# Adding the two picks' first-layer rows on VectorE in front of the second layer of a two-pick feed-forward

## The chip, the core and the metric

The kernel runs on one core of one Trainium2 chip. The metric is the device time of one execution in microseconds, as the median of several executions. The core's engines are named as the profile names them: PE is TensorE (PEld its weight loads), DVE is VectorE, ACT is ScalarE, POOL is GpSimd, SP is SyncE.

## The reference

The reference works on 2048 tokens of 128 features and runs four sub-layers in a row, each as x = x + layernorm(f(layernorm(x))): a linear attention, a feed-forward with two picked low-rank experts, an attention over 16 heads that keeps the 64 largest scores of each row, and a mixture of eight gated experts. Two of them matter here. The first feed-forward:

```python
top_v, top_i = jax.lax.top_k(scores, TOP_K)          # TOP_K = 2
val_sum = top_v.sum(axis=-1)
for e in range(E):
    count = (top_i == e).sum(axis=-1).astype(hidden_states.dtype)
    gate = count * val_sum
    inter = hidden @ wi.T + bi + (hidden @ lora_A[e].T) @ lora_B[e].T
    h = jax.nn.relu(inter)
    expert_out = h @ wo.T + bo
    out = out + gate[..., None] * expert_out
```

Both picks of a token carry the same gate and share `wo` and `bo`, so the output is val_sum * (h1 @ wo.T + h2 @ wo.T + 2 * bo), where h1 and h2 are the 512 hidden features of the first and of the second pick. The attention that comes after it selects by a threshold:

```python
topk_vals = jax.lax.top_k(dots, K)[0]                # K = 64
thresh = topk_vals[..., -1:]
dots = jnp.where(dots < thresh, NEG_INF, dots)
```

## The kernel before

All arithmetic named here is in f32 except where another type is given. The tokens are 16 tiles of 128, and the first feed-forward takes them in four blocks `b` of four tiles. One program per engine is written out by hand, and each runs its instructions in the order of the code. Results go through eight PSUM banks in a ring: the list `fills` (from `plan_fills`) names every filling of a bank in order, PE fills, and ACT or DVE empties. PE waits for the bank's last user (`open_fill`).

**First layer** (PE lines 891 and 892, function `mids`). For each block there are eight fillings `("mid", b, n)`. Number n stands for pick n // 4 and for hidden features 128 * (n % 4) and on. Each is two products over 512 tokens, and ACT drains it with bias and relu (line 579, recorded as L501, the line of the helper `drain`) into `mid[:, b % 2, n, :]`, a slice of the buffer R. The order before is n = 0, 1, ..., 7: first the four of pick 0, then the four of pick 1. Every f32 matmul stands as two matmul instructions in the profile.

**Second layer** (PE lines 902 and 903). PE waits until ACT has drained `("mid", b, 7)`, and then makes for each of the four tiles eight products of 128 x 128 x 128, which run over both picks and accumulate in PSUM, and one product of a single row that adds 2 * bo.

**Normalisation** (DVE lines 1239 to 1252). DVE scales the block by val_sum (L1242), normalises it, adds it to X (L1250) and normalises X again for the next sub-layer. ACT gives the two square roots; in ACT's order they stand ahead of the third and the sixth first-layer drain of the following block. PE transposes the normalised block behind the next block's second layer (L761), and the last block's at the end.

**The attention behind it** works in 64 groups k: tile t = k // 4, and four heads i of the sixteen, 4 * (k % 4) + i. A group is four score rows for each of 128 tokens, 16 + 128 * (t + 1) scores wide. DVE finds for every row the 56th largest of 128 candidates in f16 (`pivots`, whose first instruction is L1286) and sets a cut a little below it. ACT counts the scores above the cut; if these are 56 to 64, the threshold is the cut or one of the eight largest scores below it. A row is in doubt where the count lies outside, or where a score equals the cut bit for bit:

```python
mark(dve.scalar_tensor_tensor(out=tie[:, :], in0=r9[:, :, 1], scalar=-BIG_, in1=cutb[:, k % 2, :],
                              op0=ALU.mult, op1=ALU.is_le))
...
    mark(dve.scalar_tensor_tensor(out=doubt[:, GU * g:GU * g + GU], in0=th[rows_g, :], scalar=0.0,
                                  in1=tie[rows_g, :], op0=ALU.is_equal, op1=ALU.max))
...
with dve.If(doubtful != 0):
    settle(k)
```

One doubtful row among the 512 of a group sends DVE into `settle(k)`. It goes over the four heads in a loop and repeats an exact search for the head in doubt: a copy (L1365), then eight times MAX8 (L1368, L1372) with MATCH_REPLACE8 between them (L1370). DVE releases ACT and PE for the group's values only afterwards (line 1428, `s_lose`).

Of the kernel before, what the change touches and what calls it, by code (L numbers as in the profile page):

```python
# [5 lines left out]
ALU = mybir.AluOpType  # L6
# [4 lines left out]
P = 128  # L11
# [19 lines left out]
HALF = 2.0 ** 23  # L31
CUT = 56
CONSTS = 4 + 2 * E0 + 9
GU = 4
NG = UNITS // GU
F16 = mybir.dt.float16
# [44 lines left out]
def plan_fills():  # L81
    f = Fills()
    for n in ("wi", "wo", "loraB", "loraA_gate"):
        f.add(n, "act")
    for b in range(6):
        f.add(("wqkv", b), "act")
    f.add("memk", "act")
    f.add("memv", "act")
    for b in range(4):
        f.add(("h", 0, b), "act")  # L90
    for b in range(8):
        f.add(("kv", b), "dve")
    for b in range(4):
        f.add(("q", b), "dve")
    f.add("memscore", "act")
    f.add(("G", 0), "act")
    f.add(("G", 1), "act")
    f.add("kvsum", "dve")
    for b in range(8):
        f.add(("att", b), "dve")  # L100
    f.add(("G", 2), "act")
    f.add(("G", 3), "act")
    for g in range(4):
        f.add(("M", g), "act")
    for g in range(4):
        f.add(("MV", g), "act")
    for b in range(4):
        f.add(("h", 1, b), "act")
    f.add("logit0", "dve")
    for b in range(4):  # L110
        f.add(("lowrank", b), "dve")
    for k in range(2):
        for b in range(4):
            f.add(("pick", k, b), "act")
    for b in range(4):
        for n in range(8):
            f.add(("mid", b, n), "act")
        f.add(("ffn0", b), "dve")
        if b:
            f.add(("h", 2, b - 1), "act")  # L120
    f.add(("h", 2, 3), "act")
    return f
# [55 lines left out]
def build(nc, out, x, Wqkv, bqkv, wi, bi, wo, bo0, loraA, loraB, gate_w, gate_b, Wq, Wkv, Wo, bo1, pre, mem_k, mem_v,  # L178
          ln_w, ln_b, router_w, gw1, uw1, dw1, shg, shu, shd):
    fills, ffills, order = plan_fills(), plan_ffn1(), ffn1_order()  # L180
    with ExitStack() as ctx:
# [3 lines left out]
        def sem(name):  # L185
            return ctx.enter_context(nc.semaphore(name))
# [130 lines left out]
        s_drain_a = sem("s_drain_a")  # L317
# [5 lines left out]
        s_pk, s_pq = sem("s_pk"), sem("s_pq")  # L323
        s_kvm = sem("s_kvm")
        s_logit, s_exp = sem("s_logit"), sem("s_exp")
        s_pick = sem("s_pick")
        s_pre, s_WkS, s_mkS, s_G = sem("s_pre"), sem("s_WkS"), sem("s_mkS"), sem("s_G")
        s_out = sem("s_out")

# [160 lines left out]
        def _(act):  # L490
# [76 lines left out]
                drain(("h", 2, b), hT[:, 512 * b:512 * b + 512])  # L567

            for b in range(4):
                for n in range(8):  # L570
                    if n == 0 and b >= 2:

                        act.wait_ge(s_fill, fills.index(("ffn0", b - 2)) + 1)
                        drain_h2(b - 2)
                    if b and n == 2:
                        sqrt(2 + 2 * b, 4 * b - 4, 4 * b)
                    if b and n == 5:
                        sqrt(3 + 2 * b, 4 * b - 4, 4 * b)
                    drain(("mid", b, n), mid[:, b % 2, n, :], ACT.Relu, bias=bcol[:, 1 + n % 4:2 + n % 4])
            drain_h2(2)  # L580
# [169 lines left out]
        def _(pe):  # L750
# [134 lines left out]
            pe.wait_ge(s_drain_a, fills.drained(fills.index(("pick", 1, 3))))  # L885

            def mids(b):
                for n in range(8):
                    k = open_fill(("mid", b, n))
                    f = n % 4  # L890
                    pe.matmul(k, wiT[:, P * f:P * f + P], hT[:, 512 * b:512 * b + 512], start=True, stop=False)
                    pe.matmul(k, lBT[:, P * f:P * f + P], pickT[:, n // 4, 512 * b:512 * b + 512], start=False, stop=True)\
                        .then_inc(s_fill, 1)

            for b in range(4):
                mids(b)
                pe.wait_ge(s_drain_a, fills.drained(fills.index(("mid", b, 7))))
                k = open_fill(("ffn0", b))
                for i in range(4):
                    o = k[:, P * i:P * i + P]  # L900
                    for n in range(8):
                        pe.matmul(o, mid[:, b % 2, n, P * i:P * i + P], woT[:, n % 4, :], start=(n == 0), stop=False)
                    last = pe.matmul(o, tworow[:, :], rows[:, 264:392], start=False, stop=True)
                last.then_inc(s_fill, 1)
                if b:
                    pe.wait_ge(s_rows, 2 + b)
                    turn_block(("h", 2), b - 1)
# [180 lines left out]
        def _(dve):  # L1088
# [136 lines left out]
            for n in range(2):  # L1225
# [10 lines left out]
                    dve.wait_ge(s_drain_v, fills.drained(fills.index(("lowrank", 3))))  # L1236
                dve.sem_inc(s_pick, 1)
            for b in range(4):
                k = drained(("ffn0", b))
                for i in range(4):  # L1240
                    t = 4 * b + i
                    ins = dve.tensor_scalar(Y[:, t, :], k[:, P * i:P * i + P], sm[:, 2, t:t + 1], None, ALU.mult)  # L1242
                    if i < 3:
                        mark(ins)
                ins.then_inc(s_drain_v, 1)
                dve.wait_ge(s_dve, done[0])
                dve.wait_ge(s_drain_v, fills.drained(fills.index(("ffn0", b))))
                tiles = (4 * b, 4 * b + 4)
                normalize(Y, T1r, *tiles)
                link(dve.tensor_tensor(X[:, tiles[0]:tiles[1], :], X[:, tiles[0]:tiles[1], :], T1r[:, tiles[0]:tiles[1], :], ALU.add))  # L1250
                normalize(X, Y, *tiles)
                dve.sem_inc(s_rows, 1)
# [308 lines left out]
```

## Time and profile before

| | us |
|---|---|
| median of three executions | 2591.53 |
| lowest and highest | 2587.34, 2593.87 |
| the profiled execution | 2588.66 |
| its span (first to last instruction) | 2586.9 |

The span runs through the sub-layers one behind the other: the linear attention to about 125 us, the first feed-forward from 138 to 246 us, the selecting attention to about 2370 us, and the second feed-forward to the end. In the first feed-forward one engine's work follows another's by semaphore. In a timeline row the first number is the start, the second the duration, and a bracket holds the engine's idle time before it and what ended that. A run of instructions of one kind stands as one row with its count.

### The profile page before, as it was taken

Reading aid. Unit: us, or ns where it says so; the run is one execution under the profiler, and the core shown is the slowest. Engines: PE = TensorE matmul, PEld = TensorE weight load, DVE = VectorE, ACT = ScalarE, POOL = GpSimd, SP = SyncE. Lnnn points to the kernel's source line nnn. Section 1 sums busy time; section 2 is a strip of 40 time slices with the busy share of each in tenths; the row PEclk is TensorE's granted clock in tenths of the full one; section 3 lists DMA queues with packets and bytes.
Section 4 is the critical chain, followed back from the end, with each engine's and each line's share of the span. In section 5 each row is a group of like instructions: output and inputs, shape, how many; then the busy total and the mean of one; then the engine's idle time right before and its main releaser. Section 6 shows DMA issues by size and latency. Waiting matters only on the chain.

```text
span 2586.9 us, 34852 instructions
## 1 busy us (share of the span) xinstructions
PE 2154.9 (83%) x10150; PEld 1278.2 (49%) x10150; DVE 2145.0 (83%) x8999; ACT 1571.0 (61%) x2340; POOL 592.9 (23%) x459
## 2 busy tenths in 40 slices
PE   5998466777788478888989989999993999988997
PEld 3755343344444244545545545555551555555665
DVE  5523999999999899999998988988988998987445
ACT  2132345566666367777777777878782888874221
POOL 4200022222323122222333313313130423131000
PEclk9898667898989789999999999999996999988999
DMA  3000000000000000000000000000000000002000
GB/s 72 1 1 17 1 1 1 1 1 1 1 1 1 1 1 1 1 1 1 1 1 1 1 1 1 1 1 1 1 1 0 1 1 1 1 11 64 1 1 17
DMA packets 18211, 13.78 MB, mean 5 GB/s; under 512 B 6987, under 2 KB 15956, under 8 KB 18004
## 3 DMA queue, kind: packets, MB, share of 16 engines
q1 hardware_dynamic: 13824, 8.92, 1.3%
q10 hardware_dynamic: 4180, 2.50, 0.4%
q8 instruction: 81, 1.33, 0.2%
q14 instruction: 126, 1.03, 0.1%
HBM read 9.32 MB, written 2.10 MB: 4 GB/s over the span
## 4 chain that ended last, share of the span: by engine, by line
PE 45%; DVE 36%; ACT 10%; issue 4%; POOL 2%; DVEq 2%; SPq 1%; DMA 0%; ACTq 0%; POOLq 0%
PE bank L975 11%; DVE cand L1273 10%; PE bank L959 7%; PE bank L943 7%; DVE F L1344 5%; PE bank L1047 5%; ACT R L659 5%; PE bank L960 3%; DVE W L1303 3%; DVE W L1302 2%; PE bank L1055 2%; ACT R L609 2%; DVE R L1331 2%; DVE r L1333 2%; DVE r L1328 2%
## 5 line engine op out<-in xcount | busy, mean ns | idle before, releaser
L943 PE MATMUL bank<-hT,qT 128*128 128x512 f32 (+3 forms) x1280 | 591.4, 599 | 211.0 <-ACT R L609 122.0
L1273 DVE MAX8 cand<-R 128x8 f32<-128x12 f32 (+15 forms) x4096 | 671.6, 222 | 5.6 <-ACT R L609 5.2
L975 PE MATMUL bank<-WP,Y 128*128 128x512 f32 x1088 | 584.7, 631 | 0.5 <-ACT WP L666 0.2
L465 POOL TENSOR_TENSOR X<-R,X 128x144 f32<-128x144 f32 (+15 forms) x64 | 164.1, 2564 | 1675.3 <-ACT X L652 1675.3
L943 PEld LDWEIGHTS bank<-hT,qT 128*128 128x128 f32 x1280 | 244.9, 211 | 477.0 <-issue 197.5
L959 PE MATMUL bank<-ident,R 128*128 128x128 f32 x2176 | 436.2, 284 | 21.3 <-ACT R L659 15.9
L659 ACT ACTIVATE R<-R,negm 128x144 f32<-128x144 f32 (+15 forms) x256 | 309.6, 1211 | 186.0 <-DVEq L1428 186.0
L960 PE MATMUL bank<-nidentb,F 128*128 128x128 bf16 x2176 | 404.9, 222 | 0.0
L666 ACT ACTIVATE WP<-bank 128x512 f32<-128x512 f32 x544 | 320.7, 593 | 119.1 <-PE bank L960 108.3
L959 PEld LDWEIGHTS bank<-ident,R 128*128 128x128 f32 x2176 | 311.8, 143 | 149.9 <-issue 91.6
L609 ACT ACTIVATE R<-bank 128x1024 f32<-128x1024 f32 (+7 forms) x384 | 290.5, 771 | 137.8 <-PE bank L943 70.6
L636 ACT ACTIVATE signs<-R,cutb 128x144 int8<-128x144 f32 (+15 forms) x256 | 309.9, 1210 | 3.6
L960 PEld LDWEIGHTS bank<-nidentb,F 128*128 128x128 bf16 x2176 | 229.4, 105 | 103.2 <-issue 103.0
L1303 DVE TENSOR_TENSOR W<-W 128x256 f16<-128x256 f16 x768 | 216.2, 282 | 0.0
L1302 DVE TENSOR_TENSOR W<-W 128x256 f16<-128x256 f16 x768 | 208.1, 271 | 0.4
L975 PEld LDWEIGHTS bank<-WP,Y 128*128 128x128 f32 x1088 | 173.2, 195 | 53.4 <-issue 31.3
L1344 DVE TENSOR_SCALAR F<-R,thr 128x144 bf16<-128x144 f32 (+15 forms) x256 | 197.0, 771 | 2.1
L1331 DVE SCALAR_TENSOR_TENSOR R<-R,r 128x144 f32<-128x144 f32 (+15 forms) x128 | 183.9, 1437 | 4.5
L1333 DVE MAX8 r<-R 128x8 f32<-128x144 f32 (+15 forms) x128 | 167.9, 1312 | 4.4
L465 POOL TENSOR_TENSOR R<-R 128x144 f32<-128x144 f32 (+15 forms) x64 | 162.3, 2536 | 4.6 <-ACT R L652 4.4
L925 PE MATMUL bank<-hT,G 128*128 128x128 f32 x512 | 85.8, 319 | 87.3 <-ACT R L609 86.0
L652 ACT ACTIVATE X<-R,cutb 128x144 f32<-128x144 f32 (+15 forms) x64 | 77.6, 1213 | 91.4 <-DVE cutb L1317 91.4
(243 smaller groups left out, 2715.6 us busy)
## 6 DMA issues: line engine op xcount, KB each, us to landing
R<-in_L_attn_Wkv ACTq DMA_DIRECT2D x2, 512.0 KB, 8.4
out<-X SPq DMA_DIRECT2D x1, 1024.0 KB, 5.1
R<-in_L_ffn_gate_w SPq DMA_DIRECT2D x1, 1024.0 KB, 9.1
R<-in_L_ffn_up_w SPq DMA_DIRECT2D x1, 1024.0 KB, 11.6
out<-X SPq DMA_DIRECT2D x4, 256.0 KB, 2.3
R<-in_L_attn_Wq ACTq DMA_DIRECT2D x1, 512.0 KB, 6.8
WP<-in_L_attn_Wo ACTq DMA_DIRECT2D x1, 512.0 KB, 10.6
R<-in_L_ffn_wi SPq DMA_DIRECT2D x1, 256.0 KB
```

Source lines behind the costliest of these rows:

```text
L465: pool.tensor_tensor(OV[i - 2][:, 0:n], S[:, k % NS, i, 0:n], OV[i - 2][:, 0:n], ALU.subtract)\
L609: act.activation(S[:, k % NS, i, MEM + SC * c:MEM + SC * c + w], src[:, 0:w], ACT.Copy)\
L636: act.activation(signs[:, 0:n], S[:, k % NS, i, 0:n], ACT.Sign, bias=cutb[:, k % 2, i:i + 1], scale=BIG_, accum_out=cnt[:, k % 2, i:i + 1] ...
L659: act.activation(row, row, ACT.Exp, bias=negm[:, k % 2, i:i + 1], scale=1.0 / LOW).then_inc(s_prob, 1)
L666: act.activation(PT[:, b % 4, :], bank[4 + n % 2], ACT.Relu).then_inc(s_tdrain, 1)
L943: last = pe.matmul(to, qT[:, k % 2, i, :], hT[:, a:b], start=True, stop=b < n, skip_group_check=True)
L959: pe.transpose(to[:, P * i:P * i + P], S[:, k % NS, i, blk], ident[:, :])
L960: last = pe.matmul(to[:, P * i:P * i + P], F[:, i, blk], nidentb[:, :], start=False, stop=True, skip_group_check=True)
L975: pe.matmul(bank[6], Y[:, j, :], PT[:, (blocks_before(k) + j) % 4, :], start=(j == 0), stop=(j == k // 4))\
L1273: mark(dve.max(cand[:, :, c, i], lists(S[:, k % NS, i, 0:n], n, c)))
L1303: step = beside(step, dve.tensor_tensor(dst[:, :, 1, :], src[:, :, 0, :], src[:, :, 1, :], ALU.min))
L1344: mark(dve.tensor_scalar(F[:, i, 0:n], S[:, k % NS, i, 0:n], thr[:, i:i + 1], 4.0, ALU.is_lt, ALU.mult))
```

## The change

The two picks' hidden rows are added before the second layer: mid[n] += mid[n + 4] for n = 0 to 3, by four additions of 128 x 512 on DVE for each block. The second layer then runs over n = 0 to 3 alone, four products a tile where eight were. The bias row stays. So that additions can be made while the first layer still runs, the order of the first layer's fillings becomes 0, 4, 1, 5, 2, 6, 3, 7, in the plan, on ACT and on PE; ACT's two square roots keep their places by position. A new semaphore `s_pair` counts the additions, and PE waits for it in place of ACT's last drain.

```diff
+PAIRED = (0, 4, 1, 5, 2, 6, 3, 7)
...
     for b in range(4):
-        for n in range(8):
+        for n in PAIRED:
             f.add(("mid", b, n), "act")
...
             for b in range(4):
-                for n in range(8):
-                    if n == 0 and b >= 2:
+                for place_, n in enumerate(PAIRED):
+                    if place_ == 0 and b >= 2:
 
                         act.wait_ge(s_fill, fills.index(("ffn0", b - 2)) + 1)
                         drain_h2(b - 2)
-                    if b and n == 2:
+                    if b and place_ == 2:
                         sqrt(2 + 2 * b, 4 * b - 4, 4 * b)
-                    if b and n == 5:
+                    if b and place_ == 5:
                         sqrt(3 + 2 * b, 4 * b - 4, 4 * b)
...
             def mids(b):
-                for n in range(8):
+                for n in PAIRED:
                     k = open_fill(("mid", b, n))
...
             for b in range(4):
                 mids(b)
-                pe.wait_ge(s_drain_a, fills.drained(fills.index(("mid", b, 7))))
                 k = open_fill(("ffn0", b))
+                pe.wait_ge(s_pair, 4 * b + 4)
                 for i in range(4):
                     o = k[:, P * i:P * i + P]
-                    for n in range(8):
-                        pe.matmul(o, mid[:, b % 2, n, P * i:P * i + P], woT[:, n % 4, :], start=(n == 0), stop=False)
+                    for n in range(4):
+                        pe.matmul(o, mid[:, b % 2, n, P * i:P * i + P], woT[:, n, :], start=(n == 0), stop=False)
                     last = pe.matmul(o, tworow[:, :], rows[:, 264:392], start=False, stop=True)
...
             for b in range(4):
+                for n in range(4):
+                    dve.wait_ge(s_drain_a, fills.drained(fills.index(("mid", b, n + 4))))
+                    dve.tensor_tensor(mid[:, b % 2, n, :], mid[:, b % 2, n, :], mid[:, b % 2, n + 4, :], ALU.add)\
+                        .then_inc(s_pair, 1)
                 k = drained(("ffn0", b))
```

Lines of the changed kernel are up to five higher than before; L902 becomes L903 and L1250 becomes L1255.

PE, the last filling of block 0's first layer, its second layer and the first filling of block 1 (WP holds the weights `woT`, R holds `mid`, Zs and qT the bias row). Before:

```order
L891 MATMUL bank<-hT,WP 128x512 [waits s_drain_a]
L892 MATMUL bank<-R,WP 128x512
L902 MATMUL bank<-WP,R 128x128 [waits s_drain_a]
L902 MATMUL bank<-WP,R 128x128 x7
L903 MATMUL bank<-Zs,qT 128x128
L902 MATMUL bank<-WP,R 128x128 x8
L903 MATMUL bank<-Zs,qT 128x128
```

Changed:

```order
L892 MATMUL bank<-hT,WP 128x512 [waits s_drain_a]
L893 MATMUL bank<-R,WP 128x512
L903 MATMUL bank<-WP,R 128x128 [waits s_pair,s_drain_a]
L903 MATMUL bank<-WP,R 128x128 x3
L904 MATMUL bank<-Zs,qT 128x128
L903 MATMUL bank<-WP,R 128x128 x4
L904 MATMUL bank<-Zs,qT 128x128
```

Four products of each tile are gone, and the first one waits for `s_pair`.

DVE, from the end of block 0's normalisation to the start of block 1's. Before:

```order
L1115 RECIPROCAL rstd<-std 128x4 [waits s_std]
L1117 TENSOR_SCALAR Y<-X,mv,rstd 128x128 [waits s_dve]
L1117 TENSOR_SCALAR Y<-X,mv,rstd 128x128 x3
L1242 TENSOR_SCALAR Y<-bank,sm 128x128 [waits s_dve,s_fill]
L1242 TENSOR_SCALAR Y<-bank,sm 128x128 x3
```

Changed:

```order
L1116 RECIPROCAL rstd<-std 128x4 [waits s_std]
L1118 TENSOR_SCALAR Y<-X,mv,rstd 128x128 [waits s_dve]
L1118 TENSOR_SCALAR Y<-X,mv,rstd 128x128 x3
L1242 TENSOR_TENSOR R<-R 128x512 [waits s_dve,s_drain_a]
L1242 TENSOR_TENSOR R<-R 128x512 [waits s_drain_a] x3
L1247 TENSOR_SCALAR Y<-bank,sm 128x128 [waits s_fill]
L1247 TENSOR_SCALAR Y<-bank,sm 128x128 x3
```

The four additions of block 1 stand behind all of block 0's normalisation and ahead of block 1's.

## Rows read from the trace of the kernel before

**Rows 1.** Page, part 4: the chain that ended last.

```profile
PE 45%; DVE 36%; ACT 10%; issue 4%; POOL 2%; DVEq 2%; SPq 1%; DMA 0%; ACTq 0%; POOLq 0%
```

**Rows 2.** Windows of the second layer, a first layer, the last normalisation: busy, PEclk.

```profile
core 0: us, PE busy (x) PEld busy (x) DVE busy (x) ACT busy (x) POOL busy (x), PEclk, DMA share, GB/s
152.00:162.40 10.40, 9.65 (x73) 8.69 (x73) 0.00 (x0) 0.69 (x1) 0.00 (x0) 1.00 0.00 0
212.00:226.00 14.00, 13.83 (x33) 5.83 (x32) 6.79 (x32) 5.72 (x11) 0.00 (x0) 1.00 0.00 0
236.00:246.00 10.00, 1.96 (x10) 1.21 (x9) 7.39 (x36) 1.27 (x4) 0.00 (x0) 0.77 0.04 12
```

**Rows 3.** Timeline, end of block 0's first layer: start us, us, instruction.

```profile
152.01 0.69 ACT L501 ACTIVATE R<-bank,bcol 128x512 f32<-128x512 f32 x1 [1.03 <-PE bank L892]
...
152.75 2.05 PE L902 MATMUL bank<-WP,R 128*128 128x128 f32 x16 [0.78 <-ACT R L501]
...
154.73 0.48 PE L903 MATMUL bank<-Zs,qT 1*128 1x128 f32 x2
...
155.15 2.05 PE L902 MATMUL bank<-WP,R 128*128 128x128 f32 x16
```

**Rows 4.** Instruction groups by line, first feed-forward (137 to 247 us).

```profile
L902 PE MATMUL bank<-WP,R 128*128 128x128 f32 x256 | 32.8, 281 | 3.1 <-ACT R L501 3.1
...
L1250 DVE TENSOR_TENSOR X<-X,R 128x512 f32<-128x512 f32 x4 | 2.8, 693 | 0.1
```

**Rows 5.** Timeline, block 2's normalisation on DVE and block 3's last drain.

```profile
211.55 1.12 DVE L1242 TENSOR_SCALAR Y<-bank,sm 128x128 f32<-128x128 f32 x4 [13.44 <-PE bank L903]
...
221.75 1.11 DVE L1117 TENSOR_SCALAR Y<-X,mv,rstd 128x128 f32<-128x128 f32 x4
...
225.87 0.69 ACT L501 ACTIVATE R<-bank,bcol 128x512 f32<-128x512 f32 x1 [1.03 <-PE bank L892]
```

**Rows 6.** Timeline, DVE to PE after the last normalisation.

```profile
243.36 1.11 DVE L1117 TENSOR_SCALAR Y<-X,mv,rstd 128x128 f32<-128x128 f32 x4
...
244.59 1.12 PE L761 MATMUL bank<-ident,Y 128*128 128x128 f32 x4 [7.74 <-DVEq L1252]
```

**Rows 7.** Timeline, one kind of product at either clock level.

```profile
246.96 2.04 PE L925 MATMUL bank<-hT,G 128*128 128x128 f32 x8 [1.26 <-ACT MV L587]
...
256.47 1.16 PE L925 MATMUL bank<-hT,G 128*128 128x128 f32 x8
```

**Rows 8.** Timeline, L1286 opens each group's pivot search.

```profile
822.76 0.27 DVE L1286 TENSOR_REDUCE top<-cand 128x4 f32<-128x64 f32 x1 [0.38 <-DVE F L1344]
...
850.44 0.27 DVE L1286 TENSOR_REDUCE top<-cand 128x4 f32<-128x64 f32 x1 [0.68 <-DVE F L1344]
...
905.91 0.27 DVE L1286 TENSOR_REDUCE top<-cand 128x4 f32<-128x64 f32 x1 [3.90 <-issue]
...
936.81 0.27 DVE L1286 TENSOR_REDUCE top<-cand 128x4 f32<-128x64 f32 x1 [0.40 <-DVE F L1344]
...
966.08 0.27 DVE L1286 TENSOR_REDUCE top<-cand 128x4 f32<-128x64 f32 x1 [0.67 <-DVE F L1344]
...
1902.71 0.27 DVE L1286 TENSOR_REDUCE top<-cand 128x4 f32<-128x64 f32 x1
...
1987.19 0.27 DVE L1286 TENSOR_REDUCE top<-cand 128x4 f32<-128x64 f32 x1 [1.55 <-issue]
...
2029.94 0.27 DVE L1286 TENSOR_REDUCE top<-cand 128x4 f32<-128x64 f32 x1 [0.21 <-DVE F L1344]
```

**Rows 9.** Timeline, DVE and ACT in the exact search of tile 6.

```profile
880.33 0.64 DVE L1365 COPY R<-R 128x912 f32 x1 [1.10 <-issue]
...
905.85 1.06 ACT L659 ACTIVATE R<-R,negm 128x912 f32<-128x912 f32 x1 [29.80 <-DVEq L1428]
```

**Rows 10.** Timeline, the copy of the exact search of tile 13.

```profile
1949.08 1.10 DVE L1365 COPY R<-R 128x1808 f32 x1 [3.50 <-issue]
```

**Rows 11.** One source line: the exact search's MAX8, all its executions.

```profile
L1368 DVE MAX8 r<-R x14: 1110/1578/2046, 881.1 to 1977.7; 128x8 f32<-128x912 f32 x7, 128x8 f32<-128x1808 f32 x7
```

More of the change, by code:

```diff
@@ L325, in build @@
         s_logit, s_exp = sem("s_logit"), sem("s_exp")
-        s_pick = sem("s_pick")
+        s_pick, s_pair = sem("s_pick"), sem("s_pair")
         s_pre, s_WkS, s_mkS, s_G = sem("s_pre"), sem("s_WkS"), sem("s_mkS"), sem("s_G")
```

## The prediction

> **What bounds the kernel now.** I read the page first. The chain that ended last is PE for 45% and DVE for 36% of the span [rows 1]; it goes through the first feed-forward on PE, so time taken out there comes off the end. The windows of that stage say how: in the second layer PE is busy 9.65 of 10.40 us and DVE not at all, in a first layer PE is busy 13.83 of 14.00, DVE 6.79, ACT 5.72, all at granted clock 1.00, the level of 2.4 GHz [rows 2]. So PE is the bound in all four blocks and DVE is idle through each second layer. Behind it, in the selecting attention, DVE and its short releases to ACT and PE set the pace. There the starts of the pivot search (L1286) are some 28 to 43 us apart, with two exceptions: 55.5 us where group 26 (tile 6) is worked, and 84.5 us where group 55 (tile 13) is [rows 8]. Both hold one exact search: the source line has 14 MAX8, seven 912 wide and seven 1808 wide [rows 11].
>
> **Part 1, the products that go.** A tile's eight products are 16 recorded instructions that run from 152.75 to 154.73, where the bias row begins: 1.98 us, 0.124 each; a tile follows the one before after 2.40 us [rows 3]. There are 256 of them in all [rows 4], 128 go: 16 tiles x 8 x 0.124 = 15.8 us, all on PE's path. A tile then takes 1.41 us and a block's second layer 5.6 instead of 9.6.
>
> **Part 2, the additions that come.** 16 additions of 128 x 512 in f32 on DVE. The same form in the same stage, both operands in SBUF and in place, is L1250: 693 ns [rows 4]. The first three of a block are made while PE still runs the first layer and cost nothing, if DVE is free. In block 0 it is. In block 3 DVE's normalisation of block 2 starts at 211.55 and ends at 222.86, ACT's last drain ends at 226.56 [rows 5]; three additions take 2.1 us, so they are done by 225.0, with 1.6 us to spare. The fourth waits for the last drain and lies on the path. Today PE starts 0.05 us after that drain (152.70 to 152.75, [rows 3]). The new path is drain, 0.05, addition 0.69, and then 0.05 to PE, or 0.12 if DVE's release costs what the last normalisation's does (244.47 to 244.59, [rows 6]). That is 0.74 to 0.81 more a block; I take 0.78, since either release may apply, and 3.1 us for four. The lower bound is the addition alone, 0.69, since it needs the last drain and nothing can hide it; the upper one is all four additions behind the drain, 2.9 us a block and 11.6 in all.
>
> **Part 3, what is moved.** The new order of the first layer has the same 64 products on the same banks' ring, drained by the same ACT instructions. The square roots keep their positions, and DVE reaches the variances as early as before, since the additions stand behind the normalisation. PE's wait for the normalised block (L761) is already fulfilled when the second layer may start, as the additions follow that normalisation on DVE. Behind the new wait on PE stand only the second layer and what needs it. After the last block DVE has been idle and the closing normalisation is as long as before. Nothing here: 0.
>
> First feed-forward: 15.8 - 3.1 = 12.7 us off.
>
> **Part 4, the bits.** The change alters the rounding of the second layer: f32 sums of h1 + h2 go into four products instead of eight products into one sum. Every score of the attention behind it then moves in its last bits, and one branch hangs on bits: a row is in doubt where a score equals the cut exactly. I recomputed the sub-layers from the reference's inputs in double precision, with the kernel's lists, f16 pivot and f32 cut. Among some 32,000 rows just one has a count outside 56 to 64: tile 13, head 14, token 46, with 65 scores above the cut, the nearest score 6e-4 of the cut away. That is a third head of its group, and the trace agrees: in tile 13's search the copy starts 3.50 us after the flags, in tile 6's after 1.10 [rows 9, 10], so tile 13 skips two heads and tile 6 none. Rounding can't move that row. The search of tile 6 has no such row; but 16 rows have a score within 1e-6 of the cut, one of them in tile 6, head 8, token 81: group 26, first head, just where the trace has its search. So I read it as a tie in the last bit, and a tie doesn't outlive a new rounding but by chance.
>
> Its price is read from the starts of L1286. Group 26 takes 905.91 - 850.44 = 55.47 us, group 25 took 27.68: 27.8. Group 27 then takes 30.90 where group 28, in a wider tile, takes 29.27 [rows 8]: up to 1.6 more. ACT had stood idle 29.80 us for DVE's release [rows 9], so nothing hides it. I take 28.5 between 27.8 and 29.4. Tile 13's search costs 84.48 - 42.75 = 41.7 by the same rows, so a search costs about 2.0 us more for each tile further on: 22 in tile 3, 38 in tile 11, 40 in tile 12.
>
> How many new ties? In 60 redraws with random errors of 2e-7 on the normalised rows (plain f32 departs from double by 3.4e-7 there, and adding the picks first shifts the f32 rows by 1.7e-7), 33 had no tie, 19 one, 8 two, the old one came back once, the 65-row was there each time. Of the new ones two thirds lie in tiles 11 and 12.
>
> **The sum.** 2588.66 - 12.7 - 28.5 = 2547.5 for the profiled execution, which lies 2.9 below the median; against the median 2591.53 - 41.2 = 2550.3. I forecast 2550.
>
> **The rivals.** *One new tie.* The same draw brings one search: 2550 plus 20 to 44, in tile 11 or 12 2588 to 2590, which would look like no change though the stage is 12.7 shorter. For it speaks the count of near rows, 16 before the change too.
>
> *Two new ties, the slower side.* One search costs at most 28 + 9 x 2 = 46, which is less than the 49 that lie between 2550 and 0.3% above the median; from two on in the wide tiles it is slower: in 11 and 12, 2550 + 78 = 2628. It would show as more than 14 MAX8 on that line.
>
> *The bits don't decide.* The tile 6 search stays, because it comes from something else or falls on the same bit again: 2591.5 - 12.7 = 2578.8. For it speaks only that the trace names no cause; against it that the tie's place agrees in tile, group and head.
>
> *DVE becomes the late one.* If additions ran at twice 693 ns beside PE's and ACT's work on the same buffer, three would end at 222.86 + 4.2 = 227.0 instead of before 226.56, and each block would cost about 1.9 more than summed: in all up to 7 us, 2557. Against it: L1250 already runs beside ACT's drains and takes 693.
>
> *The clock.* PE's pause before each second layer grows from 0.78 [rows 3] to 1.6 us and the burst behind it halves. The four pauses of 0.78 left the granted clock at 1.00; it fell after the pause of 7.74 us at the end of the stage [rows 2, 6]. At the lower level, 1.2 GHz, eight equal records take 2.04 us instead of 1.16 [rows 7], a factor of 1.76; four second layers of 5.6 us would cost 17 more: 2567. I hold that the level stays. The Trainium skill, "TensorE: Matmul & The Clock Gate", section "A second HAM failure mode: psum-queue depth-cycling", speaks against the change here: small pauses between groups of products, as PE cycles through its banks, can swing the clock between its levels. By that rule the time is that rival's, by the row of the pauses it is the forecast; the trace has no pause of 1.6 us in this stage.
>
> *It doesn't do what it says.* The order shows eight products a tile before and four after, so the removal is real.
>
> **How the numbers follow.** Forecast 2550 (no tie anywhere): 0.53. One new tie, 2568 to 2595: 0.30. Two or more: 0.12. Search of tile 6 stays, 2579: 0.05. The DVE and the clock rival have 0.04 and 0.03 beside any of these, and move the forecast without changing its sign. A measurement of this kernel can tell about 0.3%, 7.8 us, from no change. Faster by more: 0.53 + 0.05, and of the single ties those in tiles up to 8, 0.05: 0.63. Within: the single ties further on, 0.24. Slower: two ties and a little of the single ones, 0.13. The range from 2545 (every cost at its lower end, and the scatter of the runs) to 2595 (one tie in a wide tile) leaves out the double ties. Single numbers in between are less likely than either end. The forecast's own range is 2545 to 2558.
>
> **What would show it.** In the changed trace: the products of the second layer are 128 records of 0.28 us mean, tiles 1.41 us apart; PE's wait before each second layer about 1.55 us, now for DVE; DVE's additions 16 x 0.69; the next sub-layer's first product 12.7 us earlier than 246.96; granted clock 1.00 through the blocks. Then MAX8 on the exact search's line seven times, 1808 wide only, and group 26 about 28 us long. If that line has 14 or more of other widths, the draw went the other way; if the same 912 wide search is there, my reading of the tie is wrong. If the stage itself is not 12 to 13 us shorter, part 1 or part 2 is.

## The result, and the profile after

| | us |
|---|---|
| changed kernel, median of four executions | 2566.53 (2555.21 to 2566.71) |
| kernel before, median of four | 2592.70 (2587.34 to 2596.04) |
| ratio, with 95% interval | 0.9894 (0.9874 to 0.9915) |
| profiled execution, changed | 2566.43, span 2564.7 |

The changed kernel is 1.1% faster. That is the forecast's direction and inside its whole range of 2545 to 2595, but 16 us above the forecast of 2550 and outside 2545 to 2558, the range that went with no tie. The profiled execution is 22.2 us shorter than that of before. Hardly any of it comes out of the feed-forward that was changed.

The changed stage first. The windows below cover the whole stage, from the first product of the first layer to the closing transposes, before and after. A row gives the stretch, its length, the busy time and the instructions of PE, PEld, DVE, ACT and POOL, and then PE's granted clock, where 1.00 is the level of 2.4 GHz and 0.50 that of 1.2 GHz:

```profile
137.97:244.59 106.62, 95.77 (x429) 59.66 (x429) 28.97 (x132) 26.14 (x44) 0.00 (x0) 0.99 0.00 1
```

```profile
140.26:245.71 105.45, 91.79 (x301) 52.45 (x301) 39.50 (x148) 26.14 (x44) 0.00 (x0) 0.86 0.00 0
```

It took 106.62 us and takes 105.45. PE has 128 matmul records fewer and is busy only 4 us less, since the granted clock is 0.86 in the mean where it was 0.99. Windows of the changed kernel show where the clock was lost:

```profile
140.00:154.00 14.00, 13.74 (x32) 6.00 (x32) 2.07 (x3) 5.02 (x8) 0.00 (x0) 1.00 0.00 0
154.00:158.00 4.00, 2.40 (x15) 1.93 (x15) 0.69 (x1) 0.69 (x1) 0.00 (x0) 0.96 0.00 0
157.80:171.30 13.50, 13.50 (x36) 8.56 (x35) 2.55 (x13) 0.69 (x1) 0.00 (x0) 0.50 0.00 0
158.00:170.00 12.00, 12.00 (x34) 8.03 (x33) 2.55 (x13) 0.69 (x1) 0.00 (x0) 0.50 0.00 0
170.00:184.00 14.00, 12.40 (x28) 5.12 (x27) 7.28 (x24) 6.39 (x10) 0.00 (x0) 0.95 0.00 0
206.00:228.00 22.00, 20.41 (x78) 11.46 (x78) 9.83 (x37) 6.28 (x11) 0.00 (x0) 1.00 0.00 1
228.00:246.00 18.00, 10.72 (x46) 8.74 (x46) 7.24 (x33) 1.01 (x3) 0.00 (x0) 0.54 0.00 0
```

Behind the pause of block 0 PE runs at 0.50 for more than 13 us, through most of the second layer and the first two of the eight fillings of block 1's first layer. The level does not fall in the pause but some 2 us behind it, when PE is busy again. Behind the pause of block 3 it falls once more. Blocks 1 and 2 keep 1.00. Before the change no block lost it:

```profile
138.00:241.00 103.00, 95.73 (x428) 59.62 (x428) 25.91 (x118) 25.94 (x43) 0.00 (x0) 1.00 0.00 1
```

The timeline of block 0's second layer, which answers to [rows 3]:

```profile
154.30 0.69 ACT L502 ACTIVATE R<-bank,bcol 128x512 f32<-128x512 f32 x1 [1.03 <-PE bank L893]
155.02 0.69 DVE L1242 TENSOR_TENSOR R<-R 128x512 f32<-128x512 f32 x1 [2.74 <-ACT R L502]
...
155.86 1.13 PE L903 MATMUL bank<-WP,R 128*128 128x128 f32 x8 [1.60 <-DVE R L1242]
...
157.33 1.75 PE L903 MATMUL bank<-WP,R 128*128 128x128 f32 x8
...
159.74 2.08 PE L903 MATMUL bank<-WP,R 128*128 128x128 f32 x8
```

and of block 2's, which kept the clock:

```profile
205.81 1.13 PE L903 MATMUL bank<-WP,R 128*128 128x128 f32 x8 [1.60 <-DVE R L1242]
...
207.28 1.16 PE L903 MATMUL bank<-WP,R 128*128 128x128 f32 x8
...
208.78 1.16 PE L903 MATMUL bank<-WP,R 128*128 128x128 f32 x8
```

The pause is 1.60 us, 0.82 more than the 0.78 of before. The four products of a tile take 1.16 us at the upper level and 2.08 at the lower. Block 2 gives the cost without a fall: a tile follows the one before after 1.50 us.

The fall's price follows from the starts of the second layers: 155.86, 183.84, 205.81 and 227.77. Block 1 to block 2 is 21.97 us. Block 0 to block 1 would be 0.39 shorter without a fall, since no transposes stand between (before: 24.36 against 24.75), so 21.58; it took 27.98: 6.4 lost. Block 3's second layer took 9.54 to its transposes where block 2's took 5.97: 3.6 lost. Together these are 10.0. The pause before the second layer and that layer itself are the same in all four blocks. What picks blocks 0 and 3 therefore lies elsewhere, and no run here shows it.

Then the selecting attention. The exact search's MAX8 stands seven times where it stood 14 times [rows 11], and the starts of L1291, the L1286 of before, show no long group there any more (compare [rows 8]):

```profile
L1373 DVE MAX8 r<-R x7: 2044/2044/2045, 1928.1 to 1955.4; 128x8 f32<-128x1808 f32 x7
```

```profile
852.28 0.27 DVE L1291 TENSOR_REDUCE top<-cand 128x4 f32<-128x64 f32 x1 [0.39 <-DVE F L1349]
...
880.00 0.27 DVE L1291 TENSOR_REDUCE top<-cand 128x4 f32<-128x64 f32 x1 [0.38 <-DVE F L1349]
...
908.07 0.27 DVE L1291 TENSOR_REDUCE top<-cand 128x4 f32<-128x64 f32 x1 [0.69 <-DVE F L1349]
```

From the first two, group 26 takes 27.72 us where it took 55.47, and group 27 takes 28.07 where it took 30.90: 30.6 us off in these two.

Elsewhere groups 36 to 41 are 6.5 us longer in sum. Group 36 and group 40, before and after:

```profile
1182.61:1215.40 32.79, 28.09 (x141) 16.16 (x139) 30.98 (x127) 24.90 (x37) 9.79 (x6) 1.00 0.00 1
...
1317.11:1352.31 35.20, 31.82 (x151) 17.93 (x149) 32.59 (x128) 26.97 (x38) 10.54 (x6) 0.95 0.00 1
```

```profile
1153.60:1188.08 34.48, 29.78 (x141) 16.75 (x139) 30.98 (x128) 25.03 (x37) 9.70 (x6) 0.95 0.00 1
...
1291.02:1328.06 37.04, 33.27 (x151) 18.21 (x149) 32.70 (x127) 27.07 (x38) 10.48 (x6) 0.91 0.00 1
```

The work is the same; PE was granted 0.05 less of its clock in group 36 and 0.04 less in group 40. This is not the change's doing. The two kernels below that leave the stage as before ("Only the bits" and "Only the cut") also take 211.4 us for the six groups, where the profile of before has 205.3 and that of the changed kernel 211.7. The account of the 22.2 us is then: 2.3 later at the stage's start (137.97 to 140.26), 1.2 off in the stage, 30.6 off at the search, 6.5 back in groups 36 to 41, and 0.8 back as the sum over the rest, where single groups differ by 1.6 less to 2.6 more.

### The profile page after: what moved, and what is told of

It is laid out like the page before. It is cut to its first block, busy times and chain, and to the rows that moved or that the text cites. A ratio compares the mean times of both kernels' runs of the same rounds, so it can differ in the third digit from the quotient of the medians.

```text
span 2564.7 us, 34512 instructions
## 1 busy us (share of the span) xinstructions
PE 2148.9 (84%) x10022; PEld 1267.2 (49%) x10022; DVE 2135.9 (83%) x8985; ACT 1570.3 (61%) x2340; POOL 592.5 (23%) x459
## 4 chain that ended last, share of the span: by engine, by line
PE 42%; DVE 35%; ACT 10%; issue 4%; POOL 2%; DVEq 1%; ACTq 0%; POOLq 0%
PE bank L976 10%; DVE cand L1278 10%; PE bank L960 7%; PE bank L944 7%; DVE F L1349 5%; ACT R L660 5%; PE bank L1048 5%; PE bank L961 3%; DVE W L1308 3%; DVE W L1307 2%; PE bank L1056 2%; ACT R L610 2%; DVE R L1336 2%; DVE r L1338 2%; DVE r L1333 2%
## 5 line engine op out<-in xcount | busy, mean ns | idle before, releaser
L466 POOL TENSOR_TENSOR X<-R,X 128x144 f32<-128x144 f32 (+15 forms) x64 | 163.7, 2558 | 1653.7 <-ACT X L653 1653.7
```

Of the source, the lines that this page charges most:

```text
L466: pool.tensor_tensor(OV[i - 2][:, 0:n], S[:, k % NS, i, 0:n], OV[i - 2][:, 0:n], ALU.subtract)\
```

## The experiments

Two questions: what lowers the granted clock, and what decides the exact search. "Stage" is always the time from the first layer's first product to the closing transposes of that kernel's profile.

### The additions without the shorter second layer

```diff
-    dve.tensor_tensor(mid[:, b % 2, n, :], mid[:, b % 2, n, :], mid[:, b % 2, n + 4, :], ALU.add)\
+    dve.tensor_tensor(T2[:, 512 * n:512 * n + 512], mid[:, b % 2, n, :], mid[:, b % 2, n + 4, :], ALU.add)\
...
-    for n in range(4):
-        pe.matmul(o, mid[:, b % 2, n, P * i:P * i + P], woT[:, n, :], start=(n == 0), stop=False)
+    for n in range(8):
+        pe.matmul(o, mid[:, b % 2, n, P * i:P * i + P], woT[:, n % 4, :], start=(n == 0), stop=False)
```

> The changed kernel with all eight products of a tile in the second layer again, in the old order 0 to 7; the additions are made as in the changed kernel and waited for, but written to scratch space that nobody reads. So PE's pause before each second layer is the changed kernel's (1.60 us), the burst behind it (9.6 us) and the bits are those of before. Stage below is from the first first-layer product to the start of the closing transposes: 106.6 us before, 105.5 changed. Theory A (the longer pause lets the granted clock fall): 106.6 + 4 x 0.82 = 109.9 if it holds, 3.6 to 6 us more for each fall, so some executions of 114 to 120 and a scatter of 10 us between executions. Rival B (the halved burst lets it fall): 109.9 every time, granted clock 1.00 in all four blocks. Theory on the search of tile 6 (a tie in the last bit): the old bits bring it back, 14 MAX8 on the exact search's line, group 26 about 55.5 us. Rival (timing or order brings it): 7 MAX8. Total 2591 + 3.3 = about 2595, with falls up to 2606.

The window of the stage, and the part of it up to the wait after the last block:

```profile
138.48:248.25 109.77, 95.64 (x428) 59.67 (x429) 39.53 (x148) 26.14 (x44) 0.00 (x0) 0.98 0.00 1
138.50:244.00 105.50, 95.63 (x428) 59.65 (x428) 35.83 (x133) 25.94 (x43) 0.00 (x0) 1.00 0.00 1
```

Stage 109.77 us, with four pauses of 1.59 to 1.60 us and no fall before the wait that follows the last block. The term of 0.78 to 0.81 us for each added wait is confirmed: 3.15 for four. The search of tile 6 is back, group 26 takes 58.12 us. So the timing of the changed kernel doesn't remove that search; its bits do. The median is 2594.34 against 2594.03 (ratio 0.9999, 0.9988 to 1.0009), so none of the 3.15 us more in the stage shows in the total; where it was given back stays open. The changed kernel lost its clock behind two of four such pauses, so one profile with none of four does not rule out that the long second layer, too, can lose it at this pause.

### Products that fill the pause

```diff
+    for n in range(6):
+        pe.matmul(k[:, 0:P], ident[:, :], woT[:, n % 4, :], start=True, stop=True, skip_group_check=True)
     pe.wait_ge(s_pair, 4 * b + 4)
```

> The changed kernel, with six products of 128 x 128 more on PE between the first and the second layer of each block, which stand ahead of the wait for the additions and whose result is overwritten. They fill the pause of 1.60 us (12 records of 0.124 = 1.49). Theory A: the granted clock stays at 1.00 in all four blocks, the stage takes 105.5 - 9.6 = about 96 us in every execution, total about 2556, with little scatter. Rival B (the short burst, not the pause): falls remain, the total stays near 2566 in most executions. Bits are the changed kernel's: 7 MAX8, all 1808 wide.

```profile
138.72:233.94 95.22, 86.81 (x348) 51.36 (x349) 39.53 (x148) 26.14 (x44) 0.00 (x0) 0.97 0.00 0
```

Stage 95.22 us, no fall, PE idle only 0.16 us before each second layer. Median 2552.61 (2548.95 to 2556.86), ratio to before 0.9839 (0.9825 to 0.9853). With 24 products more, the kernel is 14 us faster than the changed one; 10.2 us of it lie in the stage. The short second layer stayed, so it didn't lower the clock without the pause.

### Three pairs added, the fourth as two products

```diff
-    pe.wait_ge(s_pair, 4 * b + 4)
+    pe.wait_ge(s_drain_a, fills.drained(fills.index(("mid", b, 7))))
+    pe.wait_ge(s_pair, 3 * b + 3)
...
-    for n in range(4):
-        pe.matmul(o, mid[:, b % 2, n, P * i:P * i + P], woT[:, n, :], start=(n == 0), stop=False)
+    for n in (0, 1, 2, 3, 7):
+        pe.matmul(o, mid[:, b % 2, n, P * i:P * i + P], woT[:, n % 4, :], start=(n == 0), stop=False)
...
-    for n in range(4):
+    for n in range(3):
         dve.wait_ge(s_drain_a, fills.drained(fills.index(("mid", b, n + 4))))
```

> The changed kernel with only the first three pairs added; the fourth pair goes into the second layer as two products, so a tile has five products. PE waits for ACT's last drain, as before, and the additions are done by then. The pause is 0.78 us again, the burst about 6.7 us. Three products fewer at the measured 0.23 each (0.90 for four) are 0.68 a tile, 10.8 in all: stage 106.6 - 10.8 = about 96 us. Theory A: granted clock 1.00 through all blocks, every execution the same. Rival B: falls remain after the shorter burst. The bits are new: no search in tile 6, but a new tie somewhere with a chance of 4 in 10 at 20 to 44 us. Total 2554 to 2556 without one.

```profile
141.16:237.12 95.96, 84.92 (x332) 48.92 (x332) 36.77 (x144) 26.15 (x44) 0.00 (x0) 0.98 0.00 0
```

Stage 95.96 with pauses of 0.82 us and no fall, as expected: it is a second way to keep the clock. But the total is 2579.69 (2572.87 to 2584.43), since these bits bring a search too, in tile 6 again but in another group and head:

```profile
843.65 0.64 DVE L1371 COPY R<-R 128x912 f32 x1 [3.53 <-issue]
```

It stands in group 25 and starts 3.53 us after the flags, so two heads are skipped: the third head of that group, head 6. Before it was group 26 and the first head, head 8 [rows 9]. The old search was gone and a new one drawn, 27.8 us long: group 25 takes 55.45 us where it took 27.68 before.

### Only the bits

```diff
-    for n in range(8):
-        pe.matmul(o, mid[:, b % 2, n, P * i:P * i + P], woT[:, n % 4, :], start=(n == 0), stop=False)
+    for n in range(7, -1, -1):
+        pe.matmul(o, mid[:, b % 2, n, P * i:P * i + P], woT[:, n % 4, :], start=(n == 7), stop=False)
```

> The kernel before with one edit: the eight products of a tile are summed in the order 7 to 0. Same instructions, same waits, same timing of the stage (106.6 us); only the rounding differs. Theory (tie in the last bit): the search of tile 6 is gone, group 26 takes about 27.7 us, 7 MAX8 of 1808, total 2591 - 29 = 2562, unless a new tie stands elsewhere (4 in 10, 20 to 44 us, mostly in tiles 11 and 12). Rival (the search belongs to the timing, or to the data as such): 14 MAX8, 2591.

```profile
876.91 0.63 DVE L1365 COPY R<-R 128x912 f32 x1 [1.11 <-issue]
```

A miss: stage 106.62 as expected, but the search stays where it was, group 26, first head, and the total is 2592.28. Either the search wasn't a tie, or this change of rounding left that one score on the cut. The next run tells.

### Only the cut

```diff
-SLACK = 2.0 ** -14
+SLACK = 1.01 * 2.0 ** -14
```

> The kernel before with one constant changed: the slack by which the cut lies below the pivot is 1.01 times 2^-14. Bits of all scores and all timing are those of before; every cut moves by 6e-7, some hundred units in the last place, and no count changes by it except by accident. Theory (the search of tile 6 is a score equal to the cut): it is gone, group 26 takes about 27.7 us, total 29 lower, 2565, unless another tie stands at the moved cuts (4 in 10, 20 to 44 us). Rival (a count outside 56 to 64, or anything but an equality): 14 MAX8 as before, 2594. The search of tile 13 stays under both, as its count is off by a score 6e-4 of the cut away.

The exact search's MAX8 in that kernel:

```profile
L1368 DVE MAX8 r<-R x7: 2044/2044/2045, 1927.4 to 1954.8; 128x8 f32<-128x1808 f32 x7
```

The kernel before, with every score and every wait as it was and only the cuts moved by 6e-7, loses the search of tile 6 and is faster by as much: 2563.58 (2554.66 to 2566.91), ratio 0.9872 (0.9847 to 0.9896). The search of tile 13 stays. So some score of tile 6 lies within 6e-7 of its cut. That it equals the cut, and does not push a count over a bound, rests on the prediction's recomputation, which finds no count outside 56 to 64 in that tile. The recomputation was then repeated with the second layer's partial sums rounded in each order: the score of that row moves by 2 to 5 of its own last places. The products behind a score of 0.051 have magnitudes up to 0.87, where one f32 step is 16 of those last places. That the score lands on the same value again is therefore plausible, but only argued.

This kernel is also the fair partner of the changed one, since neither has the search of tile 6 and its stage is that of before (138.19 to 244.81, 106.62 us). Its 2563.58 against the changed kernel's 2566.53, and 0.9872 against 0.9894 with intervals that overlap, say that the changed feed-forward as it stands shows no gain of its own in the total.

### The shorter second layer without the pause

A burst is here the second layer of a block, PE's work behind a pause. So far neither the long pause before the long burst nor the short burst without the pause had lowered the clock. This suggested theory C: the two have to meet. This run has the short burst behind the short pause, with the second layer's products of pick 1 left out and no additions.

```diff
-    for n in range(8):
+    for n in range(4):
         pe.matmul(o, mid[:, b % 2, n, P * i:P * i + P], woT[:, n % 4, :], start=(n == 0), stop=False)
```

> The kernel before with the second layer's products of pick 1 left out, so four products a tile without any addition; PE waits only for ACT's last drain. The second layer's output lacks pick 1. Pause 0.78 us as before, burst 6.0 us as changed. The changed kernel lost its clock in blocks 0 and 3, the long pause with the long burst did not. Theory B (the short burst alone): the granted clock falls to 0.50 in some blocks, stage above 95 us. Theory C (pause of 1.60 and short burst have to meet): clock 1.00 in all blocks, stage 106.6 - 4 x 4 x 0.90 = 92.2 us, executions close together in that stage. The scores are other ones, so the exact searches say nothing here.

```profile
138.64:230.96 92.32, 81.47 (x300) 45.35 (x300) 28.98 (x132) 26.15 (x44) 0.00 (x0) 0.97 0.00 0
```

Stage 92.32 against 92.2 expected. The granted clock is 1.00 through all four blocks:

```profile
139.00:224.90 85.90, 81.11 (x300) 45.05 (x298) 23.82 (x108) 25.74 (x42) 0.00 (x0) 1.00 0.00 0
```

Behind pauses of 0.78 us the halved burst doesn't lower the clock, and four products of a tile are worth (106.62 - 92.32) / 16 = 0.89 us. The total, 2548.09, can't be compared, since the scores of the attention are other ones.

### A longer pause, with either burst

To the changed kernel, and then to the first experiment's kernel with eight products, one more addition is given to wait for:

```diff
-    pe.wait_ge(s_pair, 4 * b + 4)
+    pe.wait_ge(s_pair, 5 * b + 5)
...
+    dve.wait_ge(s_pair, 5 * b + 4)
+    dve.tensor_tensor(T2[:, 0:512], mid[:, b % 2, 3, :], mid[:, b % 2, 3, :], ALU.add).then_inc(s_pair, 1)
```

Short burst:

> The changed kernel with one more addition of 128 x 512 behind the last pair's, into scratch space, for which PE waits too. Pause about 2.35 us before each second layer, burst 6.0 us as changed; same bits as changed. Theory C: clock falls in more blocks than the changed kernel's two, three or all four; the stage would be 94.3 + 4 x 0.73 + 4 to 6 for each fall, 109 to 121 us, total 2572 to 2585, more than 2.9 above the changed kernel. Rival D (the two falls of the changed kernel's profile were chance and the pause's length within this range decides nothing): none to two falls, stage 97 to 109. 7 MAX8 by the bits.

Long burst:

> The kernel with the additions into scratch space and all eight products, with one addition more to wait for: pause 2.35 us, burst 9.6 us, bits of before. With the short burst this pause lost the clock in three of four blocks. Theory C (pause and short burst have to meet): clock 1.00 in all four blocks, stage 109.8 + 4 x 0.73 = 112.7 us. Rival A (the pause's length alone decides, and the one profile at 1.60 us with the long burst was luck): falls here too, stage 117 to 130 us. 14 MAX8 by the bits in either case.

Windows of the kernel with the short burst:

```profile
157.80:169.40 11.60, 11.60 (x35) 8.19 (x35) 2.55 (x13) 0.00 (x0) 0.00 (x0) 0.50 0.00 0
...
185.40:199.60 14.20, 14.20 (x46) 10.34 (x46) 2.55 (x13) 0.60 (x1) 0.00 (x0) 0.50 0.01 2
...
215.40:227.40 12.00, 12.00 (x44) 9.74 (x44) 1.49 (x6) 0.50 (x1) 0.00 (x0) 0.50 0.00 0
```

and of the kernel with the long burst:

```profile
154.40:166.00 11.60, 11.58 (x77) 9.66 (x78) 1.81 (x8) 0.01 (x1) 0.00 (x0) 1.00 0.01 1
...
181.00:184.00 3.00, 3.00 (x15) 2.78 (x15) 0.00 (x0) 0.00 (x0) 0.00 (x0) 0.52 0.00 0
184.00:200.00 16.00, 16.00 (x79) 10.70 (x80) 5.96 (x28) 3.44 (x6) 0.00 (x0) 1.00 0.00 1
...
235.10:241.80 6.70, 6.70 (x30) 6.16 (x29) 0.00 (x0) 0.00 (x0) 0.00 (x0) 0.50 0.01 2
```

With a pause of 2.32 us the clock falls behind all four pauses when the burst is short, each time for 12 us or more (the fourth fall shows in the closing part, 17.82 us where 14.3 would do); the stage is 122.15 us. The expectation of the long-burst run speaks of three blocks; the profile has all four. With the long burst the clock falls behind two of four pauses. In block 1 the level is back after some 3 us and in block 3 after some 7, both times inside the same burst. The first fall cost 1.6 us (block 1 to block 2 took 27.86, block 2 to block 3 26.26), the second 3.2 (12.73 us from the start of the second layer to its transposes, where block 2 took 9.55). Stage 117.44, where 112.7 was expected without falls. The total is 2602.29 (2599.85 to 2611.26), ratio 1.0032 (1.0018 to 1.0047), the only kernel here whose interval lies above that of before. So theory C, that pause and short burst must meet for a fall, was wrong in this form. The pause brings the fall. With the short burst behind it a fall lasted longer and cost more in every case here: 3.5 to 7.8 us with four products a tile, 1.6 to 3.2 with eight. The total of the short-burst kernel is 2567.70 (2558.40 to 2575.67). Its profiled execution is the slowest of them, 2575.67, only 9.2 us above the changed kernel's, though its stage is 16.7 us longer; the attention behind it, from the first to the last group, took 2008.9 us where the changed kernel's took 2015.5. Whether its quicker executions have fewer falls wasn't seen in a profile.

### The changed kernel again

> The changed kernel again, unchanged, to see how often the clock falls. Theory C: two levels of time about 11 us apart, 2555 and 2566, by whether the falls in blocks 0 and 3 happen, with more executions at the upper one; the profile shows which blocks. If all lie at 2566 the fall is fixed, if they spread evenly from 2555 to 2566 the falls are single events of 4 to 6 us each.

The stage in the profile is 105.56 us, with falls in blocks 0 and 3 again. Of its nine executions seven lie at 2566.43 to 2566.90 and two at 2555.21 and 2557.89, about 10 us lower. That is as much as the two falls cost in the stage, 10.0, but that the two quick executions are those without falls wasn't seen in a profile. The kernel with the moved cut, whose profiled stage has no fall, spreads over as much, 2554.66 to 2566.91.

### The best version, and a pause in between

The last pair's addition is cut into four of 128 x 128, one for each tile, with a wait before each tile. One kernel also fills the pause with four products, the other doesn't. The filler kernel ran again beside them.

```diff
-    pe.wait_ge(s_pair, 4 * b + 4)
+    for n in range(4):
+        pe.matmul(k[:, 0:P], ident[:, :], woT[:, n, :], start=True, stop=True, skip_group_check=True)
     for i in range(4):
+        pe.wait_ge(s_pair, 7 * b + 4 + i)
...
-    for n in range(4):
+    for n in range(3):
...
+    dve.wait_ge(s_drain_a, fills.drained(fills.index(("mid", b, 7))))
+    for i in range(4):
+        q_ = slice(P * i, P * i + P)
+        dve.tensor_tensor(mid[:, b % 2, 3, q_], mid[:, b % 2, 3, q_], mid[:, b % 2, 7, q_], ALU.add)\
+            .then_inc(s_pair, 1)
```

> The kernel of e2_filler again, beside the other two of this call: stage 95.2 us, granted clock 1.00 in all blocks, total 2549 to 2557.

> The changed kernel with the last pair's addition cut into four of 128 x 128, one per tile; PE waits before each tile for its quarter alone, and four products fill PE's pause. The path from the last drain to the second layer is a quarter of 0.29 in place of 0.69 us, so each block is 0.40 shorter than with the filler alone: stage 95.2 - 1.6 = 93.6 us, clock 1.00, total about 1.6 below the filler kernel, 2551. Rival: the later quarters or the many waits hold PE up between tiles, and the stage is not shorter than 95.2.

> As the kernel with quarters, without the filling products: pause about 1.2 us before the short burst, between 0.78 (no fall) and 1.60 (two falls). Theory C, pause and short burst meet: if 1.2 is enough for a fall, stage 93.6 plus 4 to 6 for each fall and two levels of total; if not, 93.6 in every execution and the total equals that of e10_quarters. I expect no fall, since 1.60 made only two of four.

Quarters with filler, the drain, the quarters and the first tile of block 2:

```profile
197.58 0.69 ACT L502 ACTIVATE R<-bank,bcol 128x512 f32<-128x512 f32 x1 [1.03 <-PE bank L893]
198.30 0.90 DVE L1249 TENSOR_TENSOR R<-R 128x128 f32<-128x128 f32 x4 [1.69 <-ACT R L502]
...
198.64 1.16 PE L905 MATMUL bank<-WP,R 128*128 128x128 f32 x8 [0.21 <-DVE R L1249]
```

The four blocks of the quarters without filler:

```profile
140.40:229.50 89.10, 81.29 (x300) 45.30 (x300) 36.16 (x143) 25.95 (x43) 0.00 (x0) 1.00 0.00 0
```

The three kernels (times in us):

| kernel | pause of PE | stage | median of five | ratio to before (95%) |
|---|---|---|---|---|
| filler | 0.17 | 95.23 | 2552.09 | 0.9850 (0.9830 to 0.9869) |
| quarters and filler | 0.21 | 93.62 | 2547.71 | 0.9826 (0.9807 to 0.9845) |
| quarters alone | 1.20 | 93.88 | 2549.66 | 0.9835 (0.9812 to 0.9858) |

The quarters take the expected 1.6 us out of the stage (95.23 to 93.62), and at a pause of 1.20 us the profile shows no fall without any filler. The intervals of the three ratios overlap, so the order of the three isn't shown, but all three medians are about 14 to 19 us below the changed kernel's 2566.5 to 2566.75.

## Why the prediction was right or wrong

**What bounds the stage** was right: PE, with DVE's additions beside it. DVE's normalisation doesn't reach the last pair: in block 3 the first three additions end at 225.24 and ACT's last drain at 226.9. The 16 additions took 0.69 each, as the row of L1250 said.

**Part 1** was a little too large. I gave each record that goes 0.124 us, the length of the eight products divided by 16. The measured value of four products of a tile is 0.89 to 0.90 us, not 0.99: some 0.1 us of the 1.98 stays when the products go. That makes 14.4 us instead of 15.8.

**Part 2** was right: 0.82 a block against 0.78, 3.3 in all, and the first experiment shows 3.15 alone.

**The clock** is the step that failed. I held that the level stays, with 0.03 for the rival, by the row that pauses of 0.78 leave it alone. The changed kernel lost it behind two of four pauses of 1.60. The row of 0.78 was no bound for 1.60: the blocks before have no pause between 0.78 and 7.74. The Trainium skill, "TensorE: Matmul & The Clock Gate", section "A second HAM failure mode: psum-queue depth-cycling", says that small pauses between groups of products, in a kernel that cycles through its PSUM banks, can swing the clock. The trace agrees: behind two of the pauses of 1.60 us it has stretches at 0.50. I priced the rival at 17 us, four second layers at the lower level; the profile has 10.0, from two falls, the first of which reaches into the next first layer. That the rival's 2567 is so near the measured time is chance: its price was 7 too high, and the scatter under "The base" below makes up for it. With 14.4 - 3.3 - 10.0 = 1.1 us the stage's own gain was all but gone, and the filler, which takes only the pause away, brings it back.

**Part 3** held; no wait was added by the moved order.

**Part 4** came true in its outcome: the search of tile 6 is gone, 27.75 us in its group and 2.8 in the next, against 28.5 summed. The forecast's direction was right by this alone, and in part by luck, since I gave only 0.53 to a draw without any tie. Its step "a tie doesn't outlive a new rounding but by chance" looks mis-sized, though three roundings are too few to size it anew. I gave 0.05 to its survival; of the three new roundings of the same score that ran, the reversed order kept it, the changed kernel and the three pairs lost it, and the three pairs drew a new one. A possible reason, not tested, is that the redraws with random errors took the score's own last place as its step, which is finer than the steps in which it is summed.

**The base.** The profiled execution of before started its first layer 2.3 us earlier than the changed one and had a higher clock in groups 36 to 41, 6.5 us. Neither is the change's doing, and neither was in the sum. Over the profiles of kernels with the additions the start of that first layer moves between 137.3 and 141.2 with the same code ahead of it, and the six groups take from 205.3 us (quarters alone) to 211.7. 2588.66 - 14.4 + 3.3 + 10.0 - 30.6 + 2.3 + 6.5 + 0.8 gives 2566.6, against 2566.43 measured.

## What to carry to other kernels

An addition on another engine that halves PE's products costs a pause on PE, and the pause can cost more than its length: fill it with products that are thrown away, or hand over in pieces so that it stays as short as pauses that the trace shows to be harmless. A row about a short pause says nothing of one twice as long. Where a data-dependent branch hangs on a comparison for equality, every change of rounding draws it anew, so look at the branch before giving a change the credit for the total, and compare the changed stage by itself.

## What the runs showed of the hardware that was not expected

PE's granted clock kept its level through pauses of 0.78 and 1.20 us, fell behind two of four pauses of 1.60 us and behind all four of 2.32 us in front of the short second layer. In front of the long one it kept its level in the profile at 1.60 and fell behind two of four at 2.32. The falls came between 0.3 us before PE's next product and 2 us behind it. Once at the lower level, a PE that was busy without a gap with four products and a one-row product a tile stayed there for 13 to 17 us, until the next first layer's 512-wide products had run for 2 to 6 us, while with eight products a tile it was back after some 3 and some 7 us. In the selecting attention groups 36 and 40 differ by 1.7 and 1.8 us between two profiles with the same work, with 0.05 and 0.04 of granted clock between them; the executions of the kernel before spread over 17 us (2584.63 to 2601.45).
